# Row maxima of four heads as four 32-row tiles at once, in a shared pool of five PSUM banks, with new engine orders

## The reference, cut to what matters

```python
# x (16, 224, 512); context (16, 750, 384); 16 heads of 32; 8 experts, top 2
q = x_ln @ Wq.T + bq;  k = context @ Wk.T + bk;  v = context @ Wv.T + bv
attn = softmax(einsum('bihd,bjhd->bhij', q, k) / sqrt(32))
x = x + einsum('bhij,bjhd->bihd', attn, v).reshape(B, NQ, 512) @ Wo.T + bo
...
gates = top_2_softmax(cos_scores + route_scores)          # of layernorm(x)
h = gelu(einsum('bsd,edh->bseh', x_ln2, w1) + b1)
x = x + einsum('bse,bsed->bsd', gates, einsum('bseh,ehd->bsed', h, w2) + b2)
```

## Time and profile before

| | |
|---|---|
| median of 3 runs | 1636.24 us (1633.12 to 1640.2) |
| the profiled execution: time / span | 1631.66 us / 1629.8 us |
| attention, all four engines in step | about 50 to 1300 us |
| routing, then experts | about 1300 to 1630 us |

### The profile page before, as it was taken

The page is one execution under the profiler, slowest core; times in us unless marked ns, Lnnn a source line. Parts: engine busy times, 40 slices in busy tenths (PEclk is TensorE's granted clock), DMA queues, the critical chain, the costliest instruction groups (busy, mean ns, idle before and its releaser), DMA issues.

```text
span 1629.8 us, 33266 instructions
## 1 busy us (share of the span) xinstructions
PE 1507.0 (92%) x11422; PEld 1231.5 (76%) x11422; DVE 960.8 (59%) x1465; ACT 943.4 (58%) x2055; POOL 1066.8 (65%) x897
## 2 busy tenths in 40 slices
PE   4899999999999999999999999999999754999997
PEld 4777787878787877777777777777777443888896
DVE  6556556566666565656656565656564769444443
ACT  4466666666666666656666656665665360555554
POOL 3366867676767767767677676767776521566675
PEclk9999999999999999999999999999999775999999
DMA  6665666676767676766675757676756563687785
GB/s 195 104 90 101 125 109 126 112 136 112 131 111 131 111 132 111 143 106 131 109 136 98 143 100 144 101 141 99 141 90 122 129 237 21 117 142 138 133 142 89
DMA packets 113267, 199.29 MB, mean 122 GB/s; under 512 B 19873, under 2 KB 49153, under 8 KB 112977
## 3 DMA queue, kind: packets, MB, share of 16 engines
q1 hardware_dynamic: 98864, 165.81, 55.2%
q0 software_dynamic: 14240, 31.35, 10.8%
HBM read 64.29 MB, written 38.66 MB: 63 GB/s over the span
## 4 chain that ended last, share of the span: by engine, by line
PE 61%; POOL 19%; issue 8%; DVE 5%; ACT 4%; DMA 1%; POOLq 0%; SPq 0%; DVEq 0%; ACTq 0%
POOL psum_p L509 13%; PE M L342 8%; PE M L343 8%; PE M L344 8%; PE S L1581 8%; PE X L1558 7%; PE O L1597 6%; POOL ctx_l L493 3%; ACT pr L797 2%; POOL x_res L525 2%; PE X L1829 2%; PE X L1827 2%; PE X L1828 2%; PE M L1846 2%; PE M L1848 2%
## 5 line engine op out<-in xcount | busy, mean ns | idle before, releaser
L509 POOL TENSOR_TENSOR psum_p<-psum_p,pr 125x896 f32<-125x896 f32 x254 | 536.3, 2111 | 178.8 <-ACT pr L797 155.5
L1079 DVE TENSOR_REDUCE mx<-X 128x1 f32<-128x752 f32 x448 | 421.4, 941 | 365.6 <-PE X L1558 363.5
L797 ACT ACTIVATE pr<-S 125x448 f32<-125x448 f32 x768 | 394.6, 544 | 212.2 <-PE S L1581 199.0
L1581 PEld LDWEIGHTS S<-qst,kst 128*125 128x125 f32 x1536 | 235.3, 189 | 121.1 <-ACT pr L797 64.7
L1581 PE MATMUL S<-qst,kst 128*125 128x224 f32 x1536 | 287.1, 291 | 35.4 <-ACT pr L797 31.6
L1558 PE MATMUL X<-kh_s,q_own 128*128 128x376 f32 x896 | 241.8, 351 | 5.9 <-DVE mx L1079 5.9
L1597 PE MATMUL O<-pr,v 125*32 125x224 f32 x3072 | 188.5, 364 | 1.7 <-ACT pr L797 1.7
L506 POOL TENSOR_TENSOR psum_p<-pr 125x896 f32<-125x896 f32 x64 | 135.3, 2114 | 67.5 <-ACT pr L797 67.2
L1558 PEld LDWEIGHTS X<-kh_s,q_own 128*128 128x128 f32 x896 | 145.7, 190 | 43.9 <-issue 35.7
L670 POOL DMA_INDIRECT xg<-rows_d,table_x x63 | 64.2, 1020 | 101.5 <-DVE settled L1417 58.4
L493 POOL TENSOR_TENSOR ctx_l<-ctx_r,ctx_h 128x750 fp32r<-128x750 f32 x48 | 85.3, 1807 | 68.1 <-ACT ctx_h L712 68.1
(11 more groups left out here) (238 smaller groups left out, 2976.6 us busy)
## 6 DMA issues: line engine op xcount, KB each, us to landing
kst<-kh_s SPq DMA_DIRECT2D x128, 375.0 KB, 7.8
kst<-kl_s SPq DMA_DIRECT2D x64, 375.0 KB, 10.4
ctx_r<-ctxT SPq DMA_DIRECT2D x48, 375.0 KB, 12.2
qst<-qh_s SPq DMA_DIRECT2D x128, 112.0 KB, 2.8
rows_d<-x_res SPq DMA_DIRECT2D x32, 448.0 KB, 10.9
w_l<-w SPq DMA_DIRECT2D x16, 512.0 KB, 7.2
x_ln<-x SPq DMA_DIRECT2D x17, 448.0 KB, 11.1
qst<-ql_s SPq DMA_DIRECT2D x64, 112.0 KB, 3.0
```

What stands on the lines that cost most here:

```text
L509: pool.tensor_tensor(out=total, in0=total, in1=tiles[half], op=ALU.add).then_inc(sum_step, 1)
L797: act.activation(pr[0:KP, (3 * g + p) % 2, j, :, :], S[0:KP, n % SB, 0:2 * NQ].rearrange("p (i n) -> p i n", i=2), ACT.Exp).then_inc(exp_d ...
L1079: dve.tensor_reduce(mx[:, u:u + 1], X[:, :, 0:HALF[0][1]], AX.XY, ALU.max).then_inc(max_done, 1)
L1581: last = pe.matmul(S[0:KP, n % SB, NQ * h:NQ * (h + 1)], kst[:, i, j, o:o + KP], qst[:, i, j, :], start=True, stop=True)
```

## The change

- **Maxima.** Keys are laid out by head, so that a head's keys are 32 rows in a row. `score_for_max` gives each of four heads its own row tile (32 rows) and its own bank, M's banks 0 to 3. Units 0 and 1 are 4 matmuls of 512 keys, one for each half of the queries; unit 2 is 8 matmuls of the remaining 238. So 16 matmuls a group stand where 14 stood.
- **Banks.** `X` is gone and M has five banks. Every other result has a bank fixed by a table (`bank_plan`); a unit of the maxima claims four at once, and gives two back after each of DVE's two reductions.
- **DVE.** Six reductions (four of 1024 elements, two of 952) and a small `top` replace seven of 752.
- **ACT.** `q_apart` is gone.
- **SP.** `spread_q` brings the queries' rows into head order with 4 DMAs, and `stack_k` issues 12 DMAs for the same bytes as 3 did.
- **Orders.** All four engines' lists are new.
- The root of batch 14's second layer norm moves from DVE to POOL (`LATE`).

```diff
-SB, MB = 2, 3
+SB, MB = 2, GH + 1
...
                     for row, src in ((0, kh_s), (2 * HD, kh_s), (HD, kl_s)):
-                        sp.dma_start(kst[row:row + HD, i, :, :].bitcast(F32),
-                                     src[:, i, :].bitcast(F32)).then_inc(kst_in[i], 16)
+                        for j in range(GH):
+                            sp.dma_start(kst[row:row + HD, i, j, :].bitcast(F32),
+                                         src[HD * j:HD * (j + 1), i, :].bitcast(F32)).then_inc(kst_in[i], 16)
+
+                def spread_q(g):
+                    i = g % 2
+                    sp.wait_ge(qh_done, g + 1)
+                    if g >= 2:
+                        sp.wait_ge(x_full, XU * (g - 1))
+                    for j in range(GH):
+                        sp.dma_start(q_own[HD * j:HD * (j + 1), i, :].bitcast(F32),
+                                     qh_s[j:P:GH, i, :].bitcast(F32)).then_inc(own_in[i], 16)
...
                         stack_k(g + 1)
+                    if g + 2 < GROUPS:
+                        spread_q(g + 2)
                     if t == 0 and 0 <= b - 2 < B:
                         store_xn(b - 2)
...
@@ POOL @@
                 def first(g, b):
                     add_step(g - 1, 3)
                     add_step(g - 1, 4)
-                    ln_rsqrt(b + 1)
                     add_step(g, 0)
-                    add_step(g, 1)
-                    add_step(g, 2)
                     if b < B:
                         add_bo(b - 1)
+                    add_step(g, 1)
+                    ln_rsqrt(b + 1)
+                    add_step(g, 2)
...
@@ DVE @@
+                    dve.wait_ge(x_full, XU * g + u + 1)
+                    if u < QT:
+                        dve.tensor_reduce(mx_first[0:QP, pair, u:u + 1], M[0:QP, pair, 0:FIRST_KEYS], AX.X,
+                                          ALU.max).then_inc(max_done, 1)
+                        return
...
@@ PE @@
-                    for i, (off, w) in enumerate(HALF):
-                        last = pe.matmul(X[:, i, 0:w], own_q[:, P * u:P * (u + 1)],
-                                         kh_s[:, g % 2, off:off + w], start=True, stop=True)
+                    for qt, at, off, w in parts:
+                        for j in range(GH):
+                            head = slice(HD * j, HD * (j + 1))
+                            last = pe.matmul(M[0:QP, j, at:at + w], q_own[head, g % 2, QP * qt:QP * (qt + 1)],
+                                             kh_s[head, g % 2, off:off + w], start=True, stop=True)
...
                 def second(g, b):
                     score_for_max(g + 1, 0)
+                    score(g, 0)
                     project_k(g + 2, 0)
+                    project_q(g + 2)
+                    score(g, 1)
+                    values(g - 1, 2)
                     score_for_max(g + 1, 1)
```

More of the change, by code:

```diff
@@ L110, in misc_units @@
[L110 to L115, removed]
+            order += [("V2", b + 1, 1), ("Q", g + 2, 0), ("X0", g + 1, None), ("K0", g + 2, 4), ("yT0", b - 1, 1),
+                      ("den", g - 1, 0), ("K1", g + 2, 2), ("V3", b + 1, 4), ("X1", g + 1, None), ("X2", g + 1, None),
+                      ("yT1", b - 1, 4), ("mT", g + 1, 4)]
@@ new lines, in bank_plan @@
+        if g == GROUPS - 1:
+            order.append(("b1", 0, MB - 1))
+    by_group = ("Q", "K0", "K1", "den", "mT") + MAXIMA
+    units, ahead, used, reduced = {}, {}, [0] * MB, [0] * MB
+    for kind, n, bank in order:
+        if not 0 <= n < (GROUPS if kind in by_group else B):
+            continue
+        if kind in MAXIMA:
+            ahead[kind, n] = tuple(used[:GH])
+            for k in range(GH):
+                reduced[k] = 2 * (XU * n + MAXIMA.index(kind)) + k // 2 + 1
+        else:
+            units[kind, n] = (bank, used[bank], reduced[bank])
+            used[bank] += 1
@@ L118, in attention_phase @@
+    return units, ahead
+UNITS, AHEAD = bank_plan()
 def attention_phase(nc, *args):
@@ L885, in first, with second @@
+                    exps(g, 7)
+                    exps(g, 8)
+                    o_hi(g - 1)
+                    exps(g, 9)
+                    v_out(b, 5)
+                    exps(g, 10)
+                    ln_apply(b + 1)
+                    exps(g, 11)
+                def second(g, b):
                     exps(g, 0)
+                    q_hi(g + 2)
                     k_hi(g + 2, 0)
+                    o_copy(g - 1)
                     exps(g, 1)
+                    exps(g, 2)
+                    exps(g, 3)
+                    ctx_high(b + 1)
+                    xT_part(b + 1, 0)
+                    xT_part(b + 1, 1)
+                    k_hi(g + 2, 1)
+                    exps(g, 4)
+                    exps(g, 5)
+                    o_hi(g - 1)
+                    exps(g, 6)
+                    exps(g, 7)
+                    exps(g, 8)
+                    exps(g, 9)
+                    max_out(g + 1)
+                    exps(g, 10)
+                    exps(g, 11)
@@ new lines, in third @@
+                def third(g, b):
+                    exps(g, 0)
+                    exps(g, 1)
+                    exps(g, 2)
+                    o_copy(g - 1)
+                    exps(g, 3)
+                    k_hi(g + 2, 0)
+                    exps(g, 4)
+                    exps(g, 5)
+                    exps(g, 6)
+                    o_hi(g - 1)
+                    k_hi(g + 2, 1)
+                    v_out(b + 1, 0)
+                    exps(g, 7)
+                    exps(g, 8)
+                    exps(g, 9)
+                    max_out(g + 1)
+                    q_hi(g + 2)
+                    v_out(b + 1, 1)
+                    exps(g, 10)
+                    exps(g, 11)
@@ L888, in first, with fourth @@
+                def fourth(g, b):
+                    q_hi(g + 2)
+                    v_out(b + 1, 2)
+                    exps(g, 0)
+                    y_apply(b - 1)
+                    o_copy(g - 1)
+                    exps(g, 1)
+                    k_hi(g + 2, 0)
                     exps(g, 2)
@@ L1245, in fourth @@
[L1245 to L1259 removed]
+                    top(g + 1)
@@ L1537, in project_v @@
                         claim(f"V{kt}", b)
+                    if kt == 0 and part == 0:
+                        pe.wait_ge(ctx_lo, CC * (b + 1))
                     if b == 0 and kt == 0 and part == 0:
@@ new lines, in first, with second @@
+                    project_k(g + 2, 1)
+                    score(g, 7)
+                    project_v(b, 5, 0)
+                    score(g, 8)
+                    project_v(b, 5, 1)
+                    logits(b - 2, 0)
+                    score(g, 9)
+                    score(g, 10)
+                    logits(b - 2, 1)
+                    values(g, 1)
+                    score(g, 11)
+                def second(g, b):
+                    score_for_max(g + 1, 0)
+                    score(g, 0)
```

528 lines of the change are left out of this document (227 added, 301 removed).

## The result

The changed kernel takes 1886.17 us (median of 4 runs, 1884.99 to 1889.05), the kernel before 1634.68 beside it (4 runs, 1630.57 to 1640.2): 1.1554 times as long, 95% interval 1.1533 to 1.1574. Slower was forecast, at 1774 us and at most 1870; the time lies 16 us above the range.

A forecast was written before the change was run, and what follows sets the result against it. PE's instruction list was taken to pace the attention. Terms of -24 (list), +141 (residual) and +21 us (clock) gave +138 on the profiled 1631.7, 1770, or 1774 us as median; range 1680 to 1870.

The forecast's parts named there:

- the residual's mechanism: Second group's score 1 waits for late residual load, add_bo, step 1, ln_rsqrt, ln_apply, last exponential: 10.1 us a batch, 141 us.
- the clock: After each PE stall the granted clock falls to half level: 1.5 us a stall (0 to 3), 21 us in all.
- PE's list: Cheaper maxima matmuls less added shape changes shorten PE's instruction list by 1.5 us a batch, 24 us over 16.
- The load's time: First group's residual load issued at 19.2 us, add_bo at 23.5; 13 more DMAs hardly move it.
- two limits that ended together: Before the first group's stores: SP's 16 issues end at 14.2 us, stacked keys hold the DMA engines till about 14.
- an early load: Rival: residual landed by 13.4 us, so PE's saving stands and the kernel is faster, 1612 or 1543 us; chance 0.10.
- the split would slow the DMA engines: Rival: small 32-partition stacking DMAs are slower, stores stay at 10.9 us, 6.9 more a batch, 1870 us; chance 0.10.
- Score 0 waits too: Second group: put_max behind the residual load in SP's list, issued at 19.6 us earliest; costs nothing beside the residual wait.
- DVE and banks "at nothing": Six reductions take 7.5 us for 6.6, DVE 39% idle; banks booked at nothing, 1 us a group at most.
- cheap end (rival of 0.15): Rival: four row tiles cost one matmul, 0.7 us a group; -93 for -24 us, 1705 with the residual; chance 0.15.
- changes of shape: On PE each change of tile shape costs 0.1 us; 38 a batch before, 50 after, +1.2 us a batch.

The follow-up runs named there:

- e5_top: e3_both with DVE's last step of the maxima a one-source tensor_reduce instead of a tensor_tensor of two SBUF tiles; 1643.33 us, ratio 1.0112.
- e3_both: Changed kernel with POOL's earlier first-group order (add_bo last) and put_max earlier in SP's first and third groups; 1696.09 us, ratio 1.0454.
- e2_sp: Changed kernel with only SP reordered: put_max ahead of load_res in the first group, ahead of spread_q, load_x and store_x1 in the third; 1839.13 us, 1.1305.
- e1_pool: Changed kernel with only POOL's first-group list as before: ln_rsqrt, steps 0, 1, 2, add_bo last; 1787.06 us, ratio 1.0988.
- e11_order_stats: e5_top with fourth-group work reordered on POOL, PE and ACT, SP's store_x1 ahead of spread_q, and DVE's ln_stats behind the second k_lo; 1615.57 us, 0.9904.
- e10_twice: e5_top with every maxima matmul issued twice, 32 a group for 16; 1671.66 us, ratio 1.028.

## Why the prediction was right and wrong

The direction and the residual's mechanism were right. Two steps failed and make most of the miss: the clock, a term sized at 21 us that came to 103, and the queue of SP in the third group, which had no term and cost 63.

A ledger of one batch. PE's waits are all its idle times between two fourth-group maxima; its list is the distance less the waits, at the full clock. The batch of `e5_top`, which has PE's list of the changed kernel, gives that list undisturbed, since its clock is 1.00:

```profile
611.40:690.43 79.03, 73.64 (x620) 55.48 (x619) 52.60 (x70) 43.18 (x95) 56.00 (x50) 1.00 0.48 127
```

| us a batch | before | after | `e3_both` | `e5_top` |
|---|---|---|---|---|
| distance | 78.68 | 95.44 | 84.67 | 79.03 |
| PE waits | 1.70 | 15.29 | 7.90 | 5.19 |
| the rest | 76.98 | 80.15 | 76.77 | 73.84 |

The distance grows by -3.1 (list) + 13.6 (waits) + 6.3 (80.15 less 73.84: the lower clock) = 16.8 us, where I had -1.5 + 10.1 + 1.5. As means of the third to the fifteenth batch, distance and waits are 78.9 and 1.7 before, 95.9 and 15.0 after, 82.9 and 7.5 in `e3_both` (the batch shown is one of its slowest) and 79.7 and 5.2 in `e5_top`.

The run, from the same rows of the two profiled executions (1882.2 and 1629.8 us; 252.4 apart). A stretch of PE's work at the half level is counted as half lost, which is an estimate, and PE's list of the changed kernel is taken from `e5_top`, 1144 us between the first and the last transposed maximum for 1197 before:

| us in the run, after less before | forecast | measured |
|---|---|---|
| second groups, scores 0 and 1 (the residual) | 141 | 87 |
| fourth groups, score 0 (`put_max`) | none | 63 |
| transposed maxima (`top`) | none | 38 |
| clock | 21 | 103 |
| PE's list | -24 | -53 |
| ahead of the first and behind the last maximum | none | 15 |
| sum | 138 | 253 |

- **The residual: right in mechanism, the wait sized too long.** `add_bo` starts 23.0 us after the fourth maximum (23.5 forecast), score 1 at 32.3 (33.0). PE waits 1.81 + 5.55 = 7.4 us there for my 10.1, and 6.6 on the mean, since the chain ends 0.7 us earlier and PE's own work up to score 1 takes some 2 us more than I had it (a wait of 0.62 and a slow clock in the first group). POOL's order is worth 92 us in the changed kernel and 139 with SP's mended (`e3_both` against `e2_sp`); my terms for it were 141 + 21.
- **The load's time: right, by one of two reasons and some luck.** I had two limits that ended together: SP's issues until 14.2, and the stacked keys on the DMA engines until 14 "whatever SP does". The first held: twelve issues of 0.63 us for the keys and the four of `spread_q` hold the stores until 721.62, 14.2 after the maximum. The second did not: in 2 us pieces from 711 to 719, while SP issues the keys, the share of the DMA engines is 0.57 to 0.64, for the 1.06 of the earlier trace rows, and the stores land in 4.2 us (median). So the load is late because of the new issues, not in spite of them, and one of the two grounds on which I dismissed an early load does not hold. That the split would slow the DMA engines, a rival of 0.10, was the wrong way round.
- **`put_max` in the third group: the step that failed by having no term.** I followed SP's queue in the first group only. There "Score 0 waits too ... and costs nothing" is right, as long as the other wait is there. In the third group `put_max` stands behind `spread_q`, `load_x` and `store_x1`, and nothing covers it: 3.95 us of wait in the batch shown, 63 in the run; mending SP's order is worth 41 to 87 us (`e2_sp`, and `e3_both` against `e1_pool`).
- **The clock: the step that failed by its size, and the largest miss.** I took 1.5 us a batch for one pause and 4 us at the half level (by the prices that I named, 0.43 for 0.23 us, 4 us lose 1.9). There are three pauses (1.62, 7.4 in two parts, 3.95), the clock is at its half level, 1.2 GHz, behind each for 3 to 6 us, and that costs 6.3 us in the batch shown, 103 in the run for my 21.
- **DVE and banks "at nothing": wrong by 2.4 us a batch** (1.62 + 0.82), through `top`. `e5_top` shows 56 us for it, where `e3_both` waits up to 1.85 in place of the 0.82. The reductions themselves were sized rightly (1.22 and 1.15 us).
- **PE's list: too small a credit.** Row tiles are at my cheap end (rival of 0.15): the list shortens by 3.1 us a batch, not 1.5. A unit takes 0.42 us to the next start and adds 0.23 when doubled, so its two changes of shape take some 0.1 each, as priced. The list's 3.1 is still less than the 5.8 of the cheap end, and what takes the other 2.7 was not traced. The Trainium skill ("TensorE: Matmul & The Clock Gate", Part 3) gives four row tiles of 512 columns a factor of 3.07 over one after another. The trace agrees in direction and goes further: 0.23 us for four is a factor of 4 inside a stream. So that rival came true, and its 1705 did not, since what I had left out outweighed it.

What stays open: how the clock's part divides between the pauses, since no run changes the clock alone; in `e3_both` the same wait of 1.62 to 1.64 us for `top` was followed by a fall in 6 batches of 15. What lengthens the part behind the last maximum by some 10 us was not looked into. Whether the remaining waits of `e11_order_stats` (0.9 us before a score of the third group, 0.6 for POOL's sums) can go was not tried.

## What to carry to other kernels

When a change gives an in-order queue more entries, walk every iteration type of that queue with its new neighbours, not only the one where a stall is already suspected; here the first group's stall was forecast to 0.7 us and the third group's was not seen. Price a pause on PE with the clock that follows it, read from a stretch of the same kernel; here three pauses of 1.6 to 7.4 us were followed by 3 to 6 us at half speed each. Such a price is that of its surroundings: with the longer pauses gone, the shortest of the three was no longer followed by a fall each time. A wait that costs nothing may be the cover of the next one, so take waits away in the order in which their causes come (`ln_stats` first, then the denominators), and give even a tiny instruction a look at its operands' places.

## What the runs showed of the hardware

- Splitting a transfer within SBUF from 3 DMAs of 375 KB into 12 of 94 KB, each reading 32 partitions, halved the DMA engines' busy share for the same bytes (0.68 to 0.35 at 122 and 124 GB/s), and the stores beside them landed in 3.9 us for 10.9. It costs SP 0.61 to 0.63 us a DMA of this kind, whatever the size (28 KB: 2.43 for 4; 94 KB: 5.03 for 8; before, 375 KB: 1.19 for 2; the four at 718.52 took 3.05). SP's other DMAs lie between 0.32 (the load of x_res, 726.76) and 0.71 (`put_max`, 727.12).
- Four matmuls with 32 rows, 112 weight columns and 512 moving columns, in four row tiles and four banks, take together 0.23 us in a stream (`e10_twice` against a single unit), as one of 128 rows does.
- A DVE `tensor_tensor` of 8 columns with both inputs in SBUF lasted up to 2.04 us beside a POOL step and 0.17 without; as a `tensor_reduce` of one input it lasted 0.17 us in all 64 groups (169 to 172 ns).
- Behind PE's wait of 1.62 us (707.38) the matmuls of the keys from 708.65 on stood 0.31 us apart where they stand 0.17 apart at the full clock (from 731.25 on), although PE had work again. In the changed kernel the clock fell behind this wait of 1.62 to 1.64 us in 15 batches of 15, in `e3_both` behind the same wait in 6 of 15. Behind the wait of 0.82 (757.61) the granted clock from 758 to 764 was 1.00.
